# A graph layer in four passes: query and root products moved into the key pass, denominators computed by head, edge work run further behind

## What is computed

```
xn  = layernorm(x)
sage(h, Wl, Wr, b) = (segment_sum(h[src], dst) / max(deg, 1)) @ Wl.T + h @ Wr.T + b
gnn = sage(tanh(sage(xn, W1_l, W1_r, b1)), W2_l, W2_r, b2)
q, k, v = split(xn @ w_qkv);  phi(t) = elu(t @ proj_mat) + 1       # 8 heads of 64
kv  = sum_n phi(k) v ;  z = 1 / (phi(q) . sum_n phi(k)) ;  mix = (phi(q) kv z) @ w_proj + b_proj
x2  = x + gnn + mix
out = x2 + gate * expert(layernorm(x2))                            # top 1 of 8 experts
```

## Time and profile before

| | |
|---|---|
| median of 3 runs | 2856.57 us (2851.8 to 2859.08) |
| profiled execution | 2860.02 us, its span 2858.2 us |
| PE busy | 2654.6 us (93%), 11788 matmuls |
| DVE, POOL, ACT busy | 1820.9 (64%), 1052.8 (37%), 874.2 us (31%) |
| DMA | 548 MB, 192 GB/s over the span |
| mean granted clock of TensorE | 0.969 of full |

### The profile page before, as it was taken

One profiled execution on the slowest core, in us unless ns is written; L12 is line 12 of the kernel. 1 busy time (PEld: TensorE's weight loads), 2 busy tenths in 40 slices (PEclk: granted clock), 3 DMA queues, 4 the chain that ended last, 5 costly groups with the idle time before them and its releaser, 6 DMA issues.

```text
span 2858.2 us, 36540 instructions
## 1 busy us (share of the span) xinstructions
PE 2654.6 (93%) x11788; PEld 2110.7 (74%) x11788; DVE 1820.9 (64%) x3671; ACT 874.2 (31%) x1539; POOL 1052.8 (37%) x1003
## 2 busy tenths in 40 slices
PE   2788898989899999999988999999999799999999
PEld 2566666766688888888866777777777577777777
DVE  1678778788522223222258787888888577777775
ACT  1444444444222222222222232233232132323232
POOL 1688878888300000000025555555555301111110
PEclk7899999999899999999999999999999899999999
DMA  9777787777654444444466667776665622323231
GB/s 370 239 214 228 218 257 195 198 218 203 201 202 177 177 177 182 191 186 177 178 258 207 216 224 241 236 241 217 217 214 174 244 89 89 133 88 132 88 132 44
DMA packets 160027, 548.13 MB, mean 192 GB/s; under 512 B 26184, under 2 KB 67528, under 8 KB 108768
## 3 DMA queue, kind: packets, MB, share of 16 engines
q1 hardware_dynamic: 77088, 400.26, 36.5%
q0 software_dynamic: 35840, 84.23, 14.3%
q10 hardware_dynamic: 47040, 62.92, 6.1%
HBM read 305.52 MB, written 241.83 MB: 192 GB/s over the span
## 4 chain that ended last, share of the span: by engine, by line
PE 45%; issue 29%; DMA 11%; POOL 7%; DVE 4%; ACT 2%; SPq 1%; POOLq 0%; ACTq 0%; DVEq 0%
PE bank L1128 37%; DMA agg_d<-O,eidx 9%; PE bank L1252 2%; DVE x2T_low L292 2%; PE bank L1299 1%; POOL agg_d L367 1%; POOL a_xn_rows_low L292 1%; PE bank L1154 1%; POOL G_low L292 1%; SPq L488 1%; DMA agg_d<-O 1%; POOL G L357 1%; PE bank L410 1%; PE bank L411 1%; POOL rs L653 1%
## 5 line engine op out<-in xcount | busy, mean ns | idle before, releaser
L357 POOL DMA_INDIRECT G<-y_d,esrc x80 | 85.2, 1065 | 904.3 <-issue 716.3
L1004 DVE RECIPROCAL pd<-bank 128x512 f32<-128x512 f32 x80 | 268.2, 3353 | 88.1 <-PE bank L1252 88.1
L367 POOL DMA_INDIRECT agg_d<-O,eidx x160 | 256.9, 1605 | 163.6 <-DMA agg_d<-O,eidx 105.9
L783 ACT ACTIVATE low<-bank,b1c 128x512 f32<-128x512 f32 x80 | 55.0, 688 | 531.8 <-PE bank L1128 523.7
L431 ACT COPY O<-bank 128x512 f32<-128x512 f32 x160 | 94.1, 588 | 399.6 <-PE bank L411 299.3
L292 DVE TENSOR_TENSOR hT_made_low<-low,hT_made_high 128x512 fp32r<-128x512 f32 x80 | 55.3, 691 | 233.5 <-ACT hT_made_high L789 233.5
L707 POOL TENSOR_SCALAR veps<-mv 128x1 f32<-128x1 f32 x80 | 25.1, 314 | 466.2 <-DVE mv L984 466.2
L1135 PE MATMUL bank<-ident,a_xn 128*128 128x128 f32 x320 | 57.0, 305 | 126.6 <-DVE a_xn L896 126.6
L1128 PE MATMUL bank<-xnT_high,Wq_high 128*128 128x512 f32 x320 | 157.5, 492 | 7.7 <-DMA xnT_low<-xnT_low_d 6.4
L292 POOL TENSOR_TENSOR G_low<-G,G_high_mix 128x512 fp32r<-128x512 f32 x80 | 131.2, 1640 | 81.2 <-ACT G_high_mix L424 81.2
L292 POOL TENSOR_TENSOR a_xn_rows_low<-a_xn,a_xn_rows_high 128x512 fp32r<-128x512 f32 x80 | 140.1, 1752 | 56.7 <-ACT a_xn_rows_high L735 56.7
(11 more groups left out here) (199 smaller groups left out, 8175.1 us busy)
## 6 DMA issues: line engine op xcount, KB each, us to landing
xnT_high<-xnT_high_d SPq DMA_DIRECT2D x40, 1024.0 KB, 8.8
xnT_low<-xnT_low_d SPq DMA_DIRECT2D x40, 1024.0 KB, 10.3
agg_d<-O SPq DMA_DIRECT2D x20, 1040.0 KB, 19.3
b_agg<-agg_d SPq DMA_DIRECT2D x20, 1040.0 KB, 6.8
a_x<-in_x SPq DMA_DIRECT2D x20, 1024.0 KB
xnT_high_d<-xnT_high ACTq DMA_DIRECT2D x20, 1024.0 KB
xnT_low_d<-xnT_low ACTq DMA_DIRECT2D x20, 1024.0 KB
agg_d<-zero ACTq DMA_DIRECT2D x20, 1024.0 KB
```

What stands on the lines that cost most here:

```text
L357: pool.indirect_dma_start(G[:, j, :], None, table, bass.IndirectOffsetOnAxis(ap=esrc[:, b, j:j + 1], axis=0)).then_inc(e_g[j], 16)
L367: pool.indirect_dma_start(agg, bass.IndirectOffsetOnAxis(ap=eidx[:, j, 0:1], axis=0), O[:, j, 0:width], None, compute_op=ALU.add).then_inc ...
L783: act.activation(low[:, o, :], bank[2 + o % 2][:, :], ACT.Tanh, bias=b1c[:, o:o + 1]).then_inc(b_th, 1)
L1004: dve.reciprocal(pd[:, :], bank[2][:, :]).then_inc(m_z, 1)
```

## The change

* One stage, `nodes`, makes key, query and root products from the same transposed halves: per tile 4 transposes, 2 edge matmuls, 12 key, 12 query, 12 root and 12 outer matmuls. Query phi and root product are stored to HBM tile by tile (2 x 256 KB) by SP; `xT` is not stored. The normalised tile is kept in place in `ax`.
* The key sums: POOL adds each phi(k) tile into `acc` (128x512); the 160 matmuls with `valid` go; four small matmuls with `ones` follow the stage.
* Edge lags (`LAG`): gather 2, sum 6, scatter 7 in the first stage; gather 5, high 8, sum 9, scatter 10 in the third. SP clears the second aggregate.
* `hidden`: W1_l product only; DVE adds the root product (`rin`, 1 MB per group, read back), ACT copies y out of PSUM, DVE no longer does.
* `mix`: no query product. Denominators per group: four full-precision matmuls with a 40-column `KS`, one reciprocal of 40x512, split of it, and per tile one reduced-format matmul with `E` that spreads it to 128 rows; DVE multiplies phi(q) (read back, 1 MB per group) by it. The split constants of the expert stage are prepared within the stage, and the first expert weights loaded there.

```diff
+LAG = ({"gather": 2, "stats": 4, "norm": 5, "build": 5, "high": 5, "sum": 6, "scatter": 7},
+       {"gather": 5, "build": 8, "high": 8, "sum": 9, "scatter": 10})
...
-    def keys(turn, b):
+    def nodes(turn, k):
...
+        if active(t, 7, NT):
+            turn7, k7 = lagged(turn, k, 7)
+            b7, j7 = k7 // 4, k7 % 4
+            for phase, buf, done in ((q_d, qbuf, a_qphi), (r_d, rbuf, a_re)):
+                sp.wait_ge(done, t - 6)
+                sp.dma_start(phase[2 * turn7 + b7].rearrange("p (c n) -> p c n", c=KC)[:, j7, :],
+                             buf[:, 0, j7, :]).then_inc(a_qr[j7], 16)
...
+        if active(g, 0, NG) and j == 3:
+            sp.dma_start(agg2_g[g].rearrange("p (q w) -> p q w", w=D),
+                         zs[:, None, :].bitcast(F32).to_broadcast([P, TG, D])).then_inc(s_z2, 16)
...
+    def hid_in(turn, b):
+        g = 2 * turn + b
+        sp.dma_start(flat(rin, b), r_d[g]).then_inc(b_rin[b], 16)
+        sp.dma_start(bagg[:, b].rearrange("p j w -> p (j w)"), agg1_g[g]).then_inc(b_agg[b], 16)
+    sp.dma_start(flat(rin, 0), r_d[0]).then_inc(b_rin[0], 16)
+    sp.dma_start(flat(rin, 1), r_d[1]).then_inc(b_rin[1], 16)
+    sp.wait_ge(e_sc, 16 * NT)
...
-        if active(g, 0, NG):
-            need(sp, b_tr, 4 * (g - 1))
-            sp.dma_start(bagg[:, b].rearrange("p j w -> p (j w)"), agg1_g[g]).then_inc(b_agg[b], 16)
-            need(sp, b_h, 4 * (g - 1))
+        if active(g, 1, NG):
+            sp.wait_ge(b_hl, 4 * g)
+            if active(g, -1, NG):
+                hid_in(*lagged(turn, b, -1, 2))
             for n in range(2):
-                sp.dma_start(flat(xT[n], b), xnT_d[n][g]).then_inc(b_xt[b], 16)
-        if isinstance(g, int) and g == 1:
+                sp.dma_start(hT_d[n][g - 1], flat(bhT[n])).then_inc(b_hst, 16)
+            sp.wait_ge(b_yo, 4 * g)
+            sp.dma_start(y_g[g - 1], flat(by, 1 - b)).then_inc(b_yst[1 - b], 16)
...
+        first = isinstance(g, int)
+        if active(g, 1, NG) and j == 0:
             turn1, b1_ = lagged(turn, b, 1, 2)
             need(sp, m_p, 4 * (g - 2))
             for n in range(2):
-                if isinstance(g, int) and g == 1:
-                    paced(n + 4)
                 sp.dma_start(flat(mhT[n], b1_), hT_d[n][g - 1]).then_inc(m_ht[b1_], 16)
...
+        if j == 1:
+            if active(g, 3, NG):
+                sp.wait_ge(m_po, 4 * (g - 2))
+                sp.dma_start(part_d[g - 3], flat(mx_, 1 - b)).then_inc(m_st[1 - b], 16)
+            if active(g, 1, NG):
+                turn1, b1_ = lagged(turn, b, 1, 2)
+                need(sp, m_st[b1_], 16 * turn1)
+                sp.dma_start(flat(mx_, b1_), x_g[g - 1]).then_inc(m_x[b1_], 16)
+        if active(g, -1, NG) and j == 2 and not (first and g < 1):
+            turn1, b1_ = lagged(turn, b, -1, 2)
+            sp.wait_ge(m_qz, 4 * g)
+            sp.dma_start(flat(phq[b1_]), q_d[2 * turn1 + b1_]).then_inc(m_ph[b1_], 16)
+        if active(g, 0, NG) and j == 3 and not (first and g < 2):
+            edge_load(sp, 1, turn, b)
...
+    turns(sp, mix, 8, head=3, last=1)
+    sp.wait_ge(m_qz, NT)
+    sp.dma_start(flat(fx[0]), part_d[0]).then_inc(f_p[0], 16)
...
+    sp.wait_ge(e_sc, 16 * 2 * NT)
+    sp.dma_start(flat(fa[0]), agg2_g[0]).then_inc(f_a[0], 16)
+    sp.dma_start(flat(fa[1]), agg2_g[1]).then_inc(f_a[1], 16)
...
-        if not (isinstance(t, int) and t < TG):
-            edge_gather(pool, 0, turn, k, x)
...
         edge_scatter(pool, 0, turn, k, agg1_d.ap(), AW)
...
+        if active(t, 4, NT):
+            rows = 128 if not (isinstance(t, int) and t - 4 >= NT - TG) else (N - (NP - GROUP)) // TG
+            pool.wait_ge(a_phi, t - 3)
+            need(pool, a_ks, t - 4)
+            pool.tensor_tensor(acc[0:rows, :], acc[0:rows, :], low[0:rows, k % 4, :], ALU.add
+                               ).then_inc(a_ks, 1)
         edge_low(pool, 0, turn, k)
+        edge_gather(pool, 0, turn, k, x, skip=TG)
...
+        if active(t, 6, NT):
+            turn6, k6 = lagged(turn, k, 6)
+            qr = qbuf[:, 0, k6 % 4, :]
+            act.wait_ge(a_qp, t - 5)
+            need(act, a_qr[k6 % 4], 32 * (2 * turn6 + k6 // 4))
+            act.activation(qr, bank[6][:, :], ACT.Relu, scale=-1.0).then_inc(a_qmin, 1)
+            act.wait_ge(a_qmin, t - 5)
+            act.activation(qr, qr, ACT.Exp, scale=-1.0).then_inc(a_qexp, 1)
+        edge_out(act, 0, turn, k, bank[5][:, :])
+        edge_high(act, 0, turn, k)
...
-                act.dma_start(xnT_d[n][2 * turn + b], flat(xT[n], b)).then_inc(a_st[b], 16)
-            clear(act, agg2_g, 2 * turn + b, D, s_z2)
...
+        if active(t, 6, NT):
+            turn6, k6 = lagged(turn, k, 6)
+            act.wait_ge(a_rp, t - 5)
+            need(act, a_qr[k6 % 4], 32 * (2 * turn6 + k6 // 4))
+            act.copy(rbuf[:, 0, k6 % 4, :], bank[4][:, :]).then_inc(a_re, 1)
...
+        if active(t, 6, NT):
+            qr = qbuf[:, 0, (k - 6) % 4, :]
+            dve.wait_ge(a_qexp, t - 5)
+            dve.scalar_tensor_tensor(qr, bank[6][:, :], 0.0, qr, ALU.max, ALU.add).then_inc(a_qphi, 1)
...
-                dve.wait_ge(b_y, 4 * (g - 1) + j + 1)
-                dve.tensor_copy(by[:, b1_, j, :], bank[4 + j % 2][:, :]).then_inc(b_yo, 1)
...
+        def low_of(o):
+            dve.wait_ge(b_hh, 4 * g + o + 1)
+            low_half(dve, bhT[1][:, 0, o, :], low[:, o, :], bhT[0][:, 0, o, :]).then_inc(b_hl, 1)
+        for o in range(KC):
+            if o == 0:
+                dve.wait_ge(b_rin[b], 16 * (turn + 1))
+            dve.wait_ge(b_h, 4 * g + o + 1)
+            dve.tensor_tensor(low[:, o, :], bank[2 + o % 2][:, :], rin[:, b, o, :], ALU.add
+                              ).then_inc(b_hs, 1)
+            if o >= 1:
+                low_of(o - 1)
+        low_of(KC - 1)
...
+        if active(t, 1, NT) and k % 4 == 1:
+            g = 2 * turn + k // 4
+            dve.wait_ge(m_zh, g + 1)
+            low_half(dve, zs[LOW:STACK, :], pd[LOW:STACK, :], zs[LOW:STACK, :]).then_inc(m_zl, 1)
...
+            turn3, kk = lagged(turn, k, 3)
+            dve.wait_ge(m_zb, t - 2)
+            dve.tensor_tensor(low[:, kk % 4, :], phq[kk // 4][:, 0, kk % 4, :], bank[kk % 2][:, :],
+                              ALU.mult).then_inc(m_qz, 1)
+        edge_build(dve, 1, turn, k)
+        if active(t, 0, NT) and k % 4 == 0:
+            g = 2 * turn + k // 4
+            dve.wait_ge(m_den, g + 1)
+            need(dve, m_zl, g)
+            dve.reciprocal(pd[0:STACK, :], bank[2][0:STACK, :]).then_inc(m_z, 1)
...
-        if active(t, 3, NT):
-            dve.wait_ge(m_den, t - 2)
-            need(dve, m_qz, t - 3)
-            dve.reciprocal(pd[:, :], bank[2][:, :]).then_inc(m_z, 1)
-            dve.wait_ge(m_z, t - 2)
-            lz = low[:, (k - 3) % 4, :]
-            dve.tensor_tensor(lz, lz, pd[:, :], ALU.mult).then_inc(m_qz, 1)
...
-    def keys(turn, k):
-        t, b, j = 8 * turn + k, k // 4, k % 4
-        if active(t, 0, NT):
-            pe.wait_ge(a_xn, t + 1)
-            need(pe, a_tl, t)
-            turn_tile(bank[5], axn[:, 0, j, :]).then_inc(a_tr, 1)
-        edge_pe(pe, 0, turn, k, bank[7][:, :])
+    def nodes(turn, k):
+        t = 8 * turn + k
+        if active(t, 6, NT):
+            turn6, k6 = lagged(turn, k, 6)
+            b6, j6 = k6 // 4, k6 % 4
+            cols6 = slice(j6 * P, (j6 + 1) * P)
+            if j6 == 0:
+                pe.wait_ge(a_tl, 4 * (2 * turn6 + b6 + 1))
+            need(pe, a_qphi, t - 6)
+            product(bank[6][:, :], lambda n, c: Wq[n][:, 0, c, cols6],
+                    lambda n, c: xT[n][:, b6, c, :]).then_inc(a_qp, 1)
+        if item(0, turn, k, "sum"):
+            need(pe, a_tl, t - 2 if not isinstance(t, int) else min(t - 2, NT))
+        edge_pe(pe, 0, turn, k, bank[5][:, :])
...
+            turn3, k3 = lagged(turn, k, 3)
+            b3, j3 = k3 // 4, k3 % 4
+            pe.wait_ge(a_tl, t - 2)
+            need(pe, a_phi, t - 3)
+            product(bank[7][:, :], lambda n, c: xT[n][:, b3, c, j3 * P:(j3 + 1) * P],
+                    lambda n, c: Wk[n][:, 0, c, :]).then_inc(a_kp, 1)
...
+            need(pe, a_tl, t - 2)
+            need(pe, e_o, t - 5)
+            turn_tile(bank[5], ax[:, k2 // 4, k2 % 4, :]).then_inc(a_tr, 1)
+        if active(t, 6, NT):
+            if isinstance(t, int) and t == 6:
+                pe.wait_ge(s_split, 4)
+            need(pe, a_re, t - 6)
+            product(bank[4][:, :], lambda n, c: W1r[n][:, 0, c, cols6],
+                    lambda n, c: xT[n][:, b6, c, :]).then_inc(a_rp, 1)
+        if active(t, 5, NT):
+            k5 = (k - 5) % 8
+            pe.wait_ge(a_pl, t - 4)
+            pe.wait_ge(a_xl, t - 4)
...
-            cols = slice(2, 4) if isinstance(t, int) and t - 3 >= NT - TG else slice(0, 2)
-            for n in range(2):
-                last = pe.matmul(bank[4][0:2, :], valid[:, cols],
```

(51 more changed lines are left out.)

1028 lines of the change are left out of this document (502 added, 526 removed).

## The result

The changed kernel takes 2844.95 us (median of 12 runs, 2837.52 to 2848.9) against 2856.32 (12 runs beside them): ratio 0.996, 95% interval 0.9951 to 0.9969. It is faster, by 11 us where 90 were forecast. The profiled execution took 2842.14 us, its span is 2840.3.

A forecast was written before the change was run, and what follows sets the result against it. PE was taken to bound B, C and nearly D, with POOL and its scatter chain bounding A. Changes of +276 up to B's first transposes, B -215, C with seam -147 and D -3 gave a median of 2767 us, 90 less; range 2712 to 2872.

The forecast's parts named there:

- Prices of PE: PE times read from stage B: 0.2274 us a matmul, 0.104 a transpose, 0.88 extra for a full-precision denominator matmul.
- Stage A: First stage: PE sets 11.9 us a tile, 80 tiles, ending about 1030 us; POOL needs 8.3 a tile.
- A adds instead of filling: Rival for stage A: idle share stays on top of the new products, 13.0 us a tile or more; chance 0.08.
- Stages B and D, both seams: B starts 1045, 23.5 us a group, ends 1522; D's first normalised tile 2174, D 3 us shorter, end 2769.
- Stage C's interval: Scatter to scatter in stage C: 7.7 us a tile, 608 us for 79, between PE's 7.0 and 7.9.
- pipeline slack of two steps evens out late ones: Argument for the rival that PE sets C at 7.05 us a tile, 51 us less, 2716; chance 0.18.
- the 7.9 of the sum: Stage C, four scatters a group: 4 x 5.6 + 5.25 MB x 1.5 + 4 x 0.3 = 31.5 us, 7.9 a tile.
- The turn-taking rule: Stage C: DMA engines alternate between queues, so a scatter's 4 us transfer doubles beside bulk; 8.1 us a tile, 30 us longer.
- C's start: First query product to first scatter took 19.5 us before; 5 us added, so first scatter of C at 1547.
- Losses between: Rival, 2800 to 2848 us: slower ramp, late x load or mean, or turn-taking between DMA queues; chance 0.17.
- The scatter chain at 9.3: Rival for stage C: scatters set 9.3 us a tile or more, 126 us more, 2893; chance 0.12.
- The signs of error: Wrong if PE idles over 5% in A, DVE awaits B's aggregate after first groups, or C's interval is 7.1 or over 8.8.

The follow-up runs named there:

- a_no_root: Changed kernel with 11 of the 12 matmuls of each root product in stage A left out: 2683.03 us, ratio 0.9389, A's interval 9.65 us.
- c_qz_later: Changed kernel with stage C's qz_high copy (ScalarE) and qz_low (VectorE) a step later: 2801.95 us, ratio 0.9803, interval 7.94 us.
- c_best_small: c_best with each scatter of stage C adding only the first 32 of 512 columns (work left out): 2801.58 us, ratio 0.9806, interval 7.93 us.
- c_high_first: Changed kernel with G_high made at the head of ScalarE's step in stage C, before the reciprocal and qz copies: 2825.79 us, ratio 0.9875.
- c_all: Changed kernel, stage C: m_x add behind edge build, G_high first, qz a step later, scatter at end of GpSimd's step: 2805.16 us, ratio 0.981.
- c_all_ramp: c_all with denominators at the end of PE's step, first edge lists and second phi load ahead of B's last waits: 2794.16 us, ratio 0.9777.
- c_build: c_qz_later with VectorE's edge build at the head of its step in stage C: 2810.88 us, ratio 0.9851, interval 7.98 us.
- c_build_ramp: c_build with denominators at the end of PE's step, first edge lists and second phi load ahead of B's last waits: 2806.52 us, ratio 0.9824.
- c_pool_order: Changed kernel with stage C's scatter at the end of GpSimd's step instead of its head: 2846.5 us, ratio 0.9968.
- c_best: c_all_ramp with the scatter back at the head of GpSimd's step: 2814.85 us, ratio 0.9857, interval 8.14 us.

## Why the prediction was wrong in size, step by step

- **Prices of PE** held. With orders free and small scatters a tile of C took 7.12 us, where 7.0 was worked out; a group of B 23.5.
- **Stage A** held: PE is full, 11.68 for 11.9. The rival that A adds instead of filling is out: a_no_root shows the new matmuls at nearly their full price, so no idle share was kept on top. Behind it the next bound stands at 9.65, above the 8.3 that I gave for GpSimd's own work, and still 2 us below PE.
- **Stages B and D, both seams** held within 5 us. VectorE waited for the aggregate in nearly every group, but PE didn't wait behind it.
- **Stage C's interval** is the step that failed: 7.7 us forecast, 8.45 measured, 59 us. Its sum treated landings as the only thing beside PE (31.5 us a group) and put the order of waits among the in-order engines at nothing without a reason; the one sentence on it, that "pipeline slack of two steps evens out late ones", stood in favour of a rival. The runs showed in its place 0.5 us a tile for the order of waits (c_qz_later, 7.94, some 40 us). The rest, 0.24 a tile or 19 us, is about what I gave away by taking 7.7 and not the 7.9 of the sum. The lower clock after each stall, for which I had no term either, is part of both (30 us of 560 in the changed kernel).
- **How good the 7.9 was** is less clear than it looks. With the qz copy later, 7.94, 8.00 and 7.98 were measured, but so was 7.93 with small scatters in c_best_small, where an order held it, and the price per MB in the sum came out at 0.9 to 1.4 instead of 1.5. That the sum's 7.9 is the bound of landings is not shown; luck may have a part in it.
- **What I overlooked.** I had read the lags of stages A and B user by user, and those of C only for the loads. ScalarE's wait for the qz buffer (`need(act, m_p, ...)`) asks for the product of the same step. It stood in the kernel before too, where it cost nothing (1600 to 2200 us, PE busy all through):

```profile
ACT qz_high L808 <- PE bank L1128: 72.4, 15, 4.8
```

  There ScalarE made G_high ahead of it. The change put G_high behind it, which reading the two kernels shows. c_high_first puts G_high ahead again (24 us); c_qz_later takes the wait for the same step's product away (45 us).
- **The turn-taking rule** of the Trainium skill (DMA: Bandwidth & Descriptors, Queues, rings and completion order) gave 8.1. The kernels with the qz copy later lie about my 7.9, at 7.87 to 8.0 in c_qz_later, c_all, c_all_ramp, c_build and c_build_ramp, so these runs don't part the two. The fall of 0.8 us a group for 0.94 MB is smaller than either gives (1.4, and about 1.6: four scatters at 4 us over 3 of 31 us of bulk); the 1.3 us by the ratios isn't.
- **C's start** failed by 24 us. I scaled the start of the kernel before, in which the first scatter stands four steps behind the first query product. Now it stands ten steps in, the first eight have no product, and each hangs on a chain of other engines. PE's rows show it:

```profile
1527.38 1.04 PE L1285 MATMUL bank<-z_halves,head_expand 128*128 128x512 f32 x2 [4.93 <-DVE z_halves L313]
...
1541.56 0.77 PE L1285 MATMUL bank<-z_halves,head_expand 128*128 128x512 f32 x1 [4.95 <-DVE low L1019]
...
1548.33 5.19 PE L1277 MATMUL bank<-phi_q,KS 128*40 128x512 f32 x8 [4.09 <-DMA phi_q<-q_d]
```

  Three stalls of 4 to 5 us: the first reciprocal, the second, and the third phi load, behind which the denominators take 5.19 us at the lower clock in place of 3.63. The two edits of C's start moved the first scatter by 2 us (c_build_ramp) and 5 (c_all_ramp), the median by 4 and 11. The rest of the 24 wasn't tried.
- **The rivals.** "Losses between", 2800 to 2848, with 0.17, is where the time fell. It had named a slower ramp, which came, and late x loads, a late mean and turn-taking, none of which the runs show as the cause; an order of waits it didn't name. "The scatter chain at 9.3" had one of the two suspects at the wrong size.
- **The signs of error** pointed elsewhere. One of the three that I had named came, VectorE waiting for the aggregate in B (1090 to 1500 us, the row below), and it cost nothing, since PE was busy for 473 of 476 us. The other two didn't: PE doesn't idle in A, and the interval in C, 8.45, lies under my 8.8. GpSimd's wait for landings and PE's idle time in C (0.93 us a tile, where I had written 0.7) looked like what I had forecast. A sign set just above 7.9, the upper end of my own sum, would have caught it.

```profile
DVE rd L962 <- DMA b_agg<-agg_d: 115.5, 17, 7.6
```

**Left open.** What the landing ahead of G_low costs by itself, since c_pool_order didn't take it away. Why a scatter one place earlier costs 20 us in c_best when it cost nothing in the changed kernel, and why the edge build first gains only with small scatters. These kernels move the same waits between VectorE and GpSimd, which hold each other up (in c_build the bias add takes 1.85 us in the mean, 1.31 in the changed kernel), and no run parts these. And most of the 24 us at C's start.

## What to carry to other kernels

When a stage loses PE work, go through every in-order engine of that stage and ask for each wait how many steps lie between maker and user, and what stands behind it: a wait on the same step's product was worth 45 us here, while the one with the most microseconds in the list was worth nothing. Ask also what an edit of an order leaves standing: in a loop, the end of one step is the head of the next. A chain of landings and a chain of orders can each look like the bound; take away both before you say what either costs. And count a PE stall at more than its length where the granted clock falls behind it.

## What the runs showed of the hardware

- VectorE and GpSimd hold each other up for whole instructions: Sj 0.44 us alone and 1.96 beside G_low, eidx 0.22 and 1.83, qz_low 0.68 alone and 1.85 in the mean in c_all. The Trainium skill (SBUF — State Buffer, SBUF: two separate sides) calls the port pair that they share an exclusive lock held for the whole instruction, against a VectorE operation with two inputs in SBUF; the rows agree, even for an operation of 128x1: VectorE's m_x add and multiply, which read one operand from PSUM, stay at 0.68 us in c_all.
- After a gap of 3.47 us (1835.75 to 1839.22) PE ran 6 us at the lower level (0.43 us from matmul to matmul in place of 0.227); after one of 3.32 us (1802.43 to 1805.75) it didn't. The length of the gap doesn't tell the two apart: another of 3.32 us (1768.85 to 1772.17) was followed by the lower level, and one of 3.50 us (1904.62 to 1908.12) wasn't. These gaps and levels took 92 us of 560.
- A scatter of 32 columns, a sixteenth of the bytes, still made GpSimd wait 64.4 us in 600 for its landing (106.4 with all columns): beside bulk transfers a small scatter isn't always a fast one.
